# Four-layer graph network: another order ahead of the scatter, windows of 34, and an opening of the last layer without filler

## The chip, the cores and the metric

The kernel runs on one core of a Trainium2 chip. The metric is the device time of one execution in microseconds; the time before is the median of three runs. A core has five engines that work side by side and meet at semaphores: PE (matrix products into PSUM), DVE (vector), ACT (scalar, table functions), POOL (GpSimd) and SP, which here only issues transfers. PE's clock can be granted at 2.4 GHz (1.00 in the profile) or at half of it, 1.2 GHz (0.50).

## The reference

A graph of 625 nodes with 512 features and 20000 edges, sorted by destination, goes through four layers, each behind a layer norm and a ReLU, each added to its input:

```
h = relu(layernorm(x));  x = x + L0(h)   # GCN: D^-1/2 (A_w + I) D^-1/2 (h W_conv) + b_conv, then W_lin
h = relu(layernorm(x));  x = x + L1(h)   # SAGE: mean over in-edges @ W_l + b + h W_r, times its sigmoid
h = relu(layernorm(x));  x = x + L2(h)   # 4 transformer blocks: attention along edges + MLP,
                                         # norms conditioned on sin/cos of a noise level
h = relu(layernorm(x));  x = x + L3(h)   # GAT forward and backward, 4 heads each,
                                         # W_fuse, batch norm over nodes, relu
dst = min(int(625 * u**2), 9999), sorted # so low destinations have many edges
```

## The kernel before

All arrays stay in SBUF; nodes are padded to 640 and cut into five tiles of 128. Each engine has its own program, written out by hand in the order in which it shall run (`@block.vector`, `.scalar`, `.gpsimd`, `.tensor`, `.sync`); waits on semaphores are all that ties them. Nothing is scheduled by a planner. Products in fp32r are made of a high and a low half of each operand: ACT copies the high half (`high`), POOL subtracts it for the low half (`rest`, L1416), DVE does the same for activations.

**Preamble (0 to 33.7 us).** DVE turns the edge lists into columns, computes the norm of the five input tiles (`first_stats`, `first_norm`) and their low halves (`first_rest`), splits the edge weights into three bf16 parts (`w_part`, L2517 to L2520), and adds the bias row. ACT clears the accumulator, copies the turned tiles (`first_turned`, L1652), and computes the sine of the noise embedding. POOL computes the embedding's phase (in `mask`), the norms' inverse roots (`rstd_of`), the low halves of W_lin and W_conv, and adds the bias to x (L1464). PE turns the tiles and multiplies each by W_conv (`own_features`). SP loads the W_l and W_r tiles through a few staging slots.

**Scatter (33.7 to 118 us).** The dense weighted and unweighted adjacency is built as products of one-hot matrices. 40 groups of 512 edges: DVE makes three of the four source one-hots 128x628 (L2543), ACT the fourth (L1682, L1684), DVE the destination one-hot (L2545), `WIN` columns wide and relative to the group's lowest destination, POOL multiplies it by the three weight parts (L1483), PE makes 60 products per group (L2081 with 2 x WIN columns, twice L2084 with WIN), and DVE adds the 5 x 2 x WIN sums to the accumulator (L2554). The whole runs `passes + 1` times, passes = (widest group's span) / WIN.

**Behind it.** Degrees, their power -1/2 on POOL (L1498), scaled features, aggregation, W_lin, norm of layer 1, W_l and W_r, then the transformer blocks.

**Last layer (785.9 us on).** PE turns the mask, spreads rows of attention terms over partitions (L818), and makes the hidden features (`hidden`, 12 products each) of the forward direction. Then 8 x 5 items (n = 5 i + st): DVE the leaky-ReLU branches (L1040) and maxima (L1003) three heads ahead, POOL adds the mask (L632; for six items DVE), ACT exponentiates (L757), PE multiplies (L925) and frees the item's buffer; four buffers serve the first 15 items, six after. `idle_products` are products of a matrix of ones whose result nobody reads.

## Time and profile before

| | us |
|---|---|
| median of 3 runs | 902.62 |
| lowest, highest | 901.32, 902.70 |
| profiled execution, its own time | 900.32 |
| its span | 898.6 |
| PE busy in it | 837.1 (93%) |
| DVE busy | 644.9 (72%) |
| POOL busy | 516.5 (57%) |
| ACT busy | 459.7 (51%) |

The time of an execution and its span differ by 1.7 us, which lie outside the first and last instruction. Busy shares are averages over stages with different limits, so each edited stage has to be read by itself. The mean granted clock of PE is 0.988.

### The profile page before, as it was taken

How to read it: one execution, taken by the hardware profiler on the slowest of the kernel's cores; microseconds unless marked ns; L12 is line 12 of the kernel's file. 1: busy time of each engine (PE TensorE's matmuls, PEld its weight loads, DVE VectorE, ACT ScalarE, POOL GpSimd, SP SyncE). 2: the span in 40 equal slices, each digit the busy share in tenths (PEclk: the TensorE clock that was granted, in tenths of full speed). 3: DMA queues.
4: the chain of work that ended last, by engine and by line, in shares of the span. 5: the costliest groups of instructions: out<-in, count | busy, mean ns of one | idle time of the engine just before them, and what ended most of it. 6: DMA issues, size and time to landing. Idle time of an engine off the chain costs nothing.

```text
span 898.6 us, 18329 instructions
## 1 busy us (share of the span) xinstructions
PE 837.1 (93%) x6775; PEld 732.6 (82%) x6775; DVE 644.9 (72%) x1274; ACT 459.7 (51%) x771; POOL 516.5 (57%) x622
## 2 busy tenths in 40 slices
PE   3899999999999999999999999999999999998797
PEld 2798877779898878989887989888898988875466
DVE  8899988885575774476667366577546667689986
ACT  4787757244674233476134456424346634155664
POOL 7777744469532666743367853266684338447871
PEclk9999999999999999999999999999999999989989
DMA  5100011133200133300015310013230002100121
GB/s 135 37 0 0 0 48 26 60 102 110 59 2 5 31 109 91 109 13 2 12 44 159 89 54 12 1 36 98 81 113 20 1 1 83 36 1 31 45 60 58
DMA packets 49761, 44.34 MB, mean 49 GB/s; under 512 B 6013, under 2 KB 37439, under 8 KB 49698
## 3 DMA queue, kind: packets, MB, share of 16 engines
q1 hardware_dynamic: 47234, 39.72, 15.2%
q10 hardware_dynamic: 2464, 3.80, 1.5%
q8 instruction: 38, 0.62, 0.3%
q14 instruction: 25, 0.20, 0.1%
HBM read 42.04 MB, written 1.33 MB: 48 GB/s over the span
## 4 chain that ended last, share of the span: by engine, by line
PE 70%; DVE 16%; ACT 6%; issue 4%; DVEq 2%; POOL 1%; DMA 0%; SPq 0%; ACTq 0%
PE psum L1796 20%; PE psum L1790 18%; PE psum L1901 12%; PE psum L1871 6%; PE psum L1820 5%; PE psum L925 3%; DVE arena L2321 3%; ACT arena L1598 2%; PE psum L1844 2%; PE psum L866 1%; DVEq L2550 1%; DVE z L2543 1%; DVE arena L1003 1%; DVE stats L2444 1%; DVE hot_dst L2545 1%
## 5 line engine op out<-in xcount | busy, mean ns | idle before, releaser
L1345 POOL TENSOR_SCALAR acc<-acc,rden,flag 128x628 f32<-128x628 f32 x80 | 69.4, 868 | 119.4 <-DVE rden L2317 119.4
L1901 PE MATMUL psum<-ringw,arena 128*128 128x512 f32 (+1 forms) x480 | 119.3, 397 | 4.0 <-DVE arena L2329 2.5
L1796 PE MATMUL psum<-arena 128*128 128x384 f32 (+5 forms) x675 | 115.9, 325 | 1.1 <-DVE hot_dst L2694 1.1
L1790 PE MATMUL psum<-arena,ringw 128*128 128x314 f32 x768 | 114.2, 310 | 0.1
L1790 PEld LDWEIGHTS psum<-arena,ringw 128*128 128x128 f32 x768 | 112.9, 190 | 1.4 <-DVE arena L2294 1.1
L1796 PEld LDWEIGHTS psum<-arena 128*128 128x128 f32 (+1 forms) x675 | 104.9, 189 | 8.1 <-DVE hot_dst L2694 1.5
L1901 PEld LDWEIGHTS psum<-ringw,arena 128*128 128x128 f32 (+1 forms) x480 | 86.9, 186 | 25.6 <-DVE arena L2329 3.5
L1790 PE MATMUL psum<-arena 128*128 128x314 f32 (+1 forms) x480 | 87.8, 321 | 7.3 <-DVE arena L2321 6.7
L1790 PEld LDWEIGHTS psum<-arena 128*128 128x128 f32 (+1 forms) x480 | 70.4, 187 | 15.8 <-DVE arena L2321 14.1
L1416 POOL TENSOR_TENSOR ringw<-raw,ringw 128x512 fp32r<-128x512 f32 x56 | 71.7, 1291 | 19.3 <-ACT ringw L1639 15.4
L2294 DVE SCALAR_TENSOR_TENSOR arena<-psum,cols,arena 128x628 fp32r<-128x628 f32 x32 | 27.9, 871 | 70.6 <-ACT arena L1580 70.5
L1820 PE MATMUL psum<-ident,acc 128*128 128x128 f32 (+1 forms) x528 | 75.3, 274 | 0.2
L2321 DVE TENSOR_TENSOR arena<-psum,arena 128x640 fp32r<-128x640 f32 x80 | 65.0, 817 | 14.5 <-ACT arena L1598 14.5
L1416 POOL TENSOR_TENSOR ringw<-xn,ringw 128x512 fp32r<-128x512 f32 x49 | 64.9, 1329 | 16.2 <-ACT ringw L1639 16.1
L1483 POOL TENSOR_TENSOR hot_dst<-hot_dst,w_part 128x160 bf16<-128x160 bf16 x120 | 58.2, 512 | 26.2 <-DVE hot_dst L2545 26.2
L1593 ACT ACTIVATE acc<-acc,nsmax 128x628 f32<-128x628 f32 x80 | 65.2, 815 | 13.3 <-DVE nsmax L2312 12.9
L1820 PEld LDWEIGHTS psum<-ident,acc 128*128 128x128 f32 (+1 forms) x528 | 61.7, 140 | 8.0 <-DVE arena L2294 1.2
L1409 POOL TENSOR_SCALAR veps<-mv 128x1 f32<-128x1 f32 x60 | 13.6, 227 | 90.7 <-DVE mv L2448 89.0
L2312 DVE CUSTOM_DVE_ANT_0 acc<-psum,mask 128x628 f32<-128x628 f32 x80 | 63.7, 801 | 0.0
L1529 ACT ACTIVATE arena<-psum 128x512 fp32r<-128x512 f32 x40 | 23.8, 594 | 73.8 <-PE psum L1820 58.9
L1796 PE MATMUL psum<-arena,ringw 128*128 128x314 f32 x384 | 58.5, 310 | 2.3 <-DVE arena L2211 2.3
L1871 PE MATMUL psum<-ringw,arena 128*128 128x512 f32 x240 | 58.7, 395 | 0.9 <-DVE arena L2211 0.6
(310 smaller groups left out, 1907.0 us busy)
## 6 DMA issues: line engine op xcount, KB each, us to landing
raw<-in_L_gnn_m_w SPq DMA_DIRECT2D x16, 256.0 KB
xn<-in_L_gnn_m_w SPq DMA_DIRECT2D x16, 256.0 KB
raw<-in_L_gnn_wv SPq DMA_DIRECT2D x8, 256.0 KB
xn<-in_L_gnn_wv SPq DMA_DIRECT2D x8, 256.0 KB
raw<-in_L_gnn_wq SPq DMA_DIRECT2D x8, 256.0 KB
xn<-in_L_gnn_wq SPq DMA_DIRECT2D x8, 256.0 KB
raw<-in_L_gnn_wk SPq DMA_DIRECT2D x8, 256.0 KB
xn<-in_L_gnn_wk SPq DMA_DIRECT2D x8, 256.0 KB
```

Source lines behind the costliest of these rows:

```text
L1345: g.tensor_scalar(pbuf[:, k % 4, 0:NW], pbuf[:, k % 4, 0:NW], rden[:, k:k + 1], flag[:, 1, k % NT:k % NT + 1], ALU.mult, ALU.mult).then_in ...
L1416: g.tensor_tensor(to[1], staged[slot(n)], to[0].bitcast(F32), ALU.subtract).then_inc(split_done, 1)
L1483: ins = g.tensor_tensor(hot_dst[:, b, :, (i + 1) * WIN:(i + 2) * WIN], hot, w_part[:, i, :, bass.ds(gr, 1)].broadcast_to([P, CH, WIN]), AL ...
L1593: act.activation(pbuf[:, k % 4, 0:NW], pbuf[:, k % 4, 0:NW], ACT.Exp, bias=nsmax[:, k:k + 1], scale=-1.0, accum_out=den[:, k:k + 1]).then_ ...
L1790: ins = pe.matmul(big[buf(u)][0:l.shape[1], h, 0:HW], l, r[:, h * HW:(h + 1) * HW], start=(i == 0), stop=(i == len(terms) - 1))
L1796: ins = pe.matmul(to, l, r, start=(i == 0), stop=(i == len(terms) - 1))
L1820: ins = pe.transpose(bflat(u)[0:KEYS[k], k * P:(k + 1) * P], src[:, k * P:k * P + KEYS[k]], ident[:, :])
L1871: ins = pe.matmul(brow(u), l, r, start=(k == 0 and i == 0), stop=(k == KT - 1 and i == 2))
L1901: ins = pe.matmul(brow(ROWBLK[f"{name}{t}"])[0:KEYS[t], :], l, r, start=(pieces[0] + i == 0), stop=(pieces[-1] == KT - 1 and i == len(term ...
L2294: dve.scalar_tensor_tensor(wide(to[:, 1, h, :]), bwide(u), bqk[:, i, bass.ds(it * KT + h, 1)], wide(f32(to[:, 0, h, :])), ALU.add, ALU.sub ...
L2312: dve.tensor_tensor_reduce(wide(pbuf[:, k % 4, :]), bwide(u), wide(mask[:, t, :]), -DH ** -0.5, 3e38, ALU.add, ALU.min, nsmax[:, k:k + 1]) ...
L2321: dve.tensor_tensor(pT[:, 1, :, t * P:(t + 1) * P], bflat(u).rearrange("p (k n) -> p k n", k=NT), f32(pT[:, 0, :, t * P:(t + 1) * P]), ALU ...
```

## The change

- The window of a group is 34 destinations (`WIN`), the buffers keep room for 40 (`ROOM`).
- Preamble: POOL's sum of the phase waits for DVE's two small products; the low half of W_conv stands two steps earlier; the five bias additions leave for behind the scatter, two ahead of the degrees' power, three behind the last W_l halves. DVE splits the weights ahead of the bias row and the last two tiles, and no longer copies the diagonals (ACT does, with the ones and two W_l tiles, ahead of its third tile) nor waits for the own features before the loop. PE turns the fifth tile ahead of the embedding's product and the third own features. The W_r tiles load in another order, the first into z once the degrees are summed. Filler products: 4 becomes 2, 7 becomes 6, 1 becomes 3.
- Last layer: the fifth hidden tile stands in two halves of six products where seven products of ones stood; six of ones ahead of the loop become five; four stand at each of four places in the loop.

```diff
-WIN = 40
+WIN = 34
+ROOM = 40
...
-ACCW = NP + WIN
+ACCW = NP + ROOM
...                                            # last layer, PE
+                if p == NJ // 2 - 1:          # in target_rows(p), ahead of its wait on c_up
+                    idle_products(pe, 0, 4)
...
             hidden(3)
-
-            pe.wait_ge(h_read, 2 * NT - NROW)
-            spare = 2 * NBIG + ROW3[f"Hf{NT - 1}"] % NROW
-            idle_products(pe, spare, 1)
             target_rows(0)
-            idle_products(pe, spare, 3)
+            hidden(4, range(0, KT // 2))
             second_branch(0)
-            idle_products(pe, spare, 3)
+            hidden(4, range(KT // 2, KT))
             pe.wait_ge(am_read, 2)
             second_branch(1)
             first_branch(0)
             maxima(EARLY)
             first_branch(1)
-            hidden(4)
             pe.wait_ge(one_up, 2)
             pe.wait_ge(h_read, 2 * NT)
-            idle_products(pe, 2 * NBIG, 6)
+            idle_products(pe, 2 * NBIG, 5)
             for n in range(NJ * NT):
...
+                for p in range(1, NJ // 2):
+                    if n == 2 * NT * p - 5:
+                        pe.wait_ge(misc_read, MISC[f"vt{p}"] + 1)
+                        idle_products(pe, 0, 4)
                 pe.wait_ge(p_up, n + 1)
...                                            # SP, loads of W_r
-                elif n in Q_RIGHT[:2]:
-                    sp.wait_ge(xb_up, NT)
-                elif n >= OUTER:
+                elif n == Q_RIGHT[0]:
+                    sp.wait_ge(deg_full, 1)
+                elif n >= OUTER and n != Q_RIGHT[1]:
...                                            # POOL
             step(g.tensor_scalar(part, kf, -TURN_HI, 1.0, ALU.mult, ALU.mult))
+            g.wait_ge(dstep, 9)
             step(g.tensor_tensor(r, part, ph, ALU.add))
             rstd_of(0, 0)
             rstd_of(1, 1)
             rest(Q_LIN, ringpart(Q_LIN))
             step(g.tensor_scalar(part, kf, -float(2 * np.pi - TURN_HI), 1.0, ALU.mult, ALU.mult))
             rstd_of(2, 2)
+            rest(Q_CONV, ringpart(Q_CONV))
+            rstd_of(3, 3)
             step(g.tensor_tensor(r, r, part, ALU.add))
-            rstd_of(3, 3)
             g.tensor_scalar(r, r, 3.1415925, -3.1415925, ALU.min, ALU.max).then_inc(emb_up, 1)
             rstd_of(4, 4)
-            rest(Q_CONV, ringpart(Q_CONV))
...
             for k in range(2):
                 left_rest(k)
+            for t in range(2):
+                bias_added(t)
             g.wait_ge(w_up, 1)
...
             for k in range(2, KT):
                 left_rest(k)
+            for t in range(2, NT):
+                bias_added(t)
...                                            # ACT, behind first_turned(1)
+            act.wait_ge(scat_read, HOT)
+            act.wait_ge(scat_full, HOT)
...
+            act.activation(diag, ident[:, :].unsqueeze(1).broadcast_to([P, NT - 1, P]), ACT.Copy).then_inc(acc_up, 1)
+            act.activation(w_acc[:, NT - 1, (NT - 1) * P:NP], ident[:, :], ACT.Copy).then_inc(acc_up, 1)
+            act.activation(ones_r[:, :], ones[:, :], ACT.Copy).then_inc(ones_up, 1)
+            for m in range(2, 4):
+                high(m, ringpart(m)[0])
...                                            # DVE, ahead of the loop
-            dve.tensor_copy(diag, ident[:, :].unsqueeze(1).broadcast_to([P, NT - 1, P])).then_inc(acc_up, 1)
-            dve.tensor_copy(w_acc[:, NT - 1, (NT - 1) * P:NP], ident[:, :]).then_inc(acc_up, 1)
             dve.wait_ge(acc_up, 2)
             dve.wait_ge(w_ready, 2)
             dve.wait_ge(hot_init, 3)
-            dve.wait_ge(big_full, BIG0["hall"] + 1)
```

DVE ahead of the scatter loop, before (L2457 is a tile's norm, L2463 a turned tile's low half, L2514 the bias row, L2517 to L2520 the weight parts, L2531 and L2532 the diagonals):

```order
L2457 TENSOR_SCALAR xn<-x,mv,rstd 128x512
L2514 TENSOR_TENSOR bias<-psum,bias 128x512
L2463 SCALAR_TENSOR_TENSOR arena<-psum,arena 128x4x128
L2457 TENSOR_SCALAR xn<-x,mv,rstd 128x512
L2517 CAST w_part<-edge_col 128x160
L2519 TENSOR_TENSOR edge_col<-edge_col,w_part 128x160
L2520 CAST w_part<-edge_col 128x160
L2519 TENSOR_TENSOR edge_col<-edge_col,w_part 128x160
L2520 CAST w_part<-edge_col 128x160
L2463 SCALAR_TENSOR_TENSOR arena<-psum,arena 128x4x128 x2
L2531 COPY acc<-ident 128x4x128
L2532 COPY acc<-ident 128x128
```

The same place after (L2486 is the norm, L2492 the low half, L2550 the bias row, L2540 to L2543 the weight parts, L2555 a product for the condition):

```order
L2486 TENSOR_SCALAR xn<-x,mv,rstd 128x512
L2540 CAST w_part<-edge_col 128x160
L2542 TENSOR_TENSOR edge_col<-edge_col,w_part 128x160
L2543 CAST w_part<-edge_col 128x160
L2542 TENSOR_TENSOR edge_col<-edge_col,w_part 128x160
L2543 CAST w_part<-edge_col 128x160
L2550 TENSOR_TENSOR bias<-psum,bias 128x512
L2492 SCALAR_TENSOR_TENSOR arena<-psum,arena 128x4x128
L2486 TENSOR_SCALAR xn<-x,mv,rstd 128x512
L2492 SCALAR_TENSOR_TENSOR arena<-psum,arena 128x4x128
L2555 TENSOR_TENSOR pick<-fcol,pick 128x1
L2492 SCALAR_TENSOR_TENSOR arena<-psum,arena 128x4x128
```

The weight parts stand ahead of the bias row and the fifth norm, and the copies of the diagonal are gone.

PE at the opening of the last layer, before (L1796 hidden features, L1807 products of ones, L843 the turned target rows, L818 rows spread over partitions, L925 the weighted products of the loop):

```order
L1796 MATMUL psum<-ringw,arena 128x256 x12
L1807 MATMUL psum<-ones_r 128x512
L843 MATMUL psum<-ident,iota 36x128 x5
L1807 MATMUL psum<-ones_r 128x512 x3
L818 MATMUL psum<-arena 128x314 x2
L1807 MATMUL psum<-ones_r 128x512 x3
L818 MATMUL psum<-arena 128x314 x8
L1796 MATMUL psum<-ringw,arena 128x256 x12
L1807 MATMUL psum<-ones_r 128x512 x6
L925 MATMUL psum<-hot_dst,acc 128x314 x4
```

After (L821, L854, L827, L1834 and L935 in the same roles):

```order
L821 MATMUL psum<-ringw,arena 128x256 x12
L854 MATMUL psum<-ident,iota 36x128 x5
L821 MATMUL psum<-ringw,arena 128x256 x6
L827 MATMUL psum<-arena 128x314 x2
L821 MATMUL psum<-ringw,arena 128x256 x6
L827 MATMUL psum<-arena 128x314 x8
L1834 MATMUL psum<-ones_r 128x512 x5
L935 MATMUL psum<-hot_dst,acc 128x314 x4
```

The twelve products of the fifth tile stand around the second spread, and nothing but five products of ones is left between the last spread and the loop.

PE in the loop ahead of the last pair of heads, after:

```order
L935 MATMUL psum<-raw,acc 128x314 x2
L1834 MATMUL psum<-ones_r 128x512 x4
L854 MATMUL psum<-ident,iota 36x128 x5
L935 MATMUL psum<-hot_dst,acc 128x314 x2
L1834 MATMUL psum<-ones_r 128x512 x4
L935 MATMUL psum<-hot_dst,acc 128x314 x2
```

Both fours of L1834 are new there; the other rows keep their order.

## Rows read from the trace of the kernel before

**Rows 1.** The page's part 4, the chain by engine, share of the span.

```profile
PE 70%; DVE 16%; ACT 6%; issue 4%; DVEq 2%; POOL 1%; DMA 0%; SPq 0%; ACTq 0%
```

**Rows 2.** Busy time, ten scatter groups: PE, PEld, DVE, ACT, POOL, clock, DMA, GB/s.

```profile
61.08:81.40 20.32, 18.79 (x604) 18.01 (x601) 20.32 (x51) 15.37 (x21) 14.45 (x31) 1.00 0.00 0
```

**Rows 3.** Timeline, DVE ahead of the scatter: start, duration, engine, line, operation, [idle before].

```profile
8.97 1.57 DVE L2442 TENSOR_SCALAR xn<-ident,mnmx 40x40 f32<-40x40 f32 x1
...
23.89 1.21 DVE L2520 CAST w_part<-edge_col 128x160 bf16<-128x160 f32 x1
...
28.99 0.69 DVE L2463 SCALAR_TENSOR_TENSOR arena<-psum,arena 128x512 fp32r<-128x512 f32 x1 [0.73 <-ACT arena L1652]
...
33.72 0.97 DVE L2543 TENSOR_SCALAR mask<-iota,edge_col 128x628 bf16<-128x628 f16 x3 [2.92 <-issue]
```

**Rows 4.** Waits of DVE, 785 to 898 us: total, times, longest.

```profile
DVE hot_dst L1040 <- PE psum L925: 3.4, 3, 2.6
...
DVE raw L1040 <- PE psum L925: 0.6, 2, 0.4
```

**Rows 5.** Busy time of PE and granted clock, two stretches of the last layer.

```profile
802.90:809.70 6.80, 6.24 (x19) 0.51 0.00 1
854.00:860.60 6.60, 6.60 (x14) 0.50 0.42 128
```

**Rows 6.** Timeline, the other engines ahead of the scatter.

```profile
8.98 1.52 POOL L1441 TENSOR_TENSOR mask<-mask 64x640 f32<-64x640 f32 x1
...
21.54 1.28 POOL L1416 TENSOR_TENSOR ringw<-raw,ringw 128x512 fp32r<-128x512 f32 x1
...
23.62 6.41 POOL L1464 TENSOR_TENSOR x<-x,bias 128x512 f32<-128x512 f32 x5
...
22.97 2.05 PE L1796 MATMUL psum<-ringw,arena 128*128 128x256 f32 x8 [1.89 <-DVE arena L2463]
...
30.30 2.16 PE L1796 MATMUL psum<-ringw,arena 128*128 128x256 f32 x16
...
21.12 0.60 ACT L1652 ACTIVATE arena<-psum 128x512 fp32r<-128x512 f32 x1 [4.26 <-PE psum L1820]
...
28.29 0.60 ACT L1652 ACTIVATE arena<-psum 128x512 fp32r<-128x512 f32 x1 [1.78 <-PE psum L1820]
```

**Rows 7.** DMA issues to 130 us: count, KB each, median us to landing.

```profile
bias<-in_L_gnn_W_r SPq DMA_DIRECT2D x2, 256.0 KB, 2.8
```

**Rows 8.** Groups by line, DVE, 62 to 102 us: busy us, mean ns, idle before.

```profile
L2543 DVE TENSOR_SCALAR mask<-iota,edge_col 128x628 bf16<-128x628 f16 x30 | 14.0, 519 | 0.0
...
L2554 DVE TENSOR_TENSOR acc<-psum,acc 128x400 f32 x20 | 11.2, 560 | 0.0
L2545 DVE TENSOR_TENSOR hot_dst<-iota,edge_col 128x160 bf16<-128x160 f16 x20 | 6.2, 311 | 0.0
```

**Rows 9.** Timeline, POOL and DVE behind the scatter.

```profile
120.17 1.97 POOL L1498 TENSOR_TENSOR degs<-degs,half 128x2 f32<-128x2 f32 x2 [2.56 <-DVE degs L2609]
126.06 2.54 POOL L1416 TENSOR_TENSOR ringw<-raw,ringw 128x512 fp32r<-128x512 f32 x2 [3.92 <-DVE arena L2584]
...
132.69 0.51 DVE L2457 TENSOR_SCALAR xn<-x,mv,rstd 128x512 f32<-128x512 f32 x1
```

**Rows 10.** Timeline, opening of the last layer's loop: PE, ACT, POOL.

```profile
805.35 2.90 PE L1807 MATMUL psum<-ones_r 128*128 128x512 f32 x6 [0.56 <-ACT acc L659]
...
805.10 1.52 ACT L757 ACTIVATE hot_dst<-hot_dst,edge_col 128x628 f32<-128x628 f32 x2
...
802.38 3.02 POOL L632 TENSOR_TENSOR hot_dst<-hot_dst,acc 128x628 f32<-128x628 f32 x2 [1.50 <-issue]
```

**Rows 11.** Timeline, PE's gaps in the loop.

```profile
834.66 1.30 PE L925 MATMUL psum<-raw,acc 128*128 128x314 f32 x4 [2.04 <-ACT z L693]
...
849.32 0.71 PE L843 MATMUL psum<-ident,iota 128*36 128x128 f32 x5 [1.59 <-DVE iota L1025]
...
853.12 1.62 PE L925 MATMUL psum<-hot_dst,acc 128*128 128x314 f32 x4 [2.04 <-ACT z L693]
```

77 lines of the change are left out of this document (43 added, 34 removed).

## The prediction

> **What bounds the kernel now.** I read the page's chain of waits first, then busy time by stage, then the timeline of each engine around the edited places, and last who waited for whom and the granted clock. The chain is 70% PE, 16% DVE [rows 1]: over most of the run PE sets the pace, and the change does not touch that part. It touches three stages in which PE does not set the pace, and a short one behind the scatter.
>
> In the scatter (33.7 to 118 us) DVE has no idle time: in a stretch of ten groups it is busy 20.32 of 20.32 us, PE 18.79, ACT 15.37, POOL 14.45 [rows 2]. A group is 2.03 us of DVE. What starts DVE earlier, or makes a group of its work shorter, moves the end; PE has 0.15 us a group to spare.
>
> Ahead of the scatter DVE's last product of the preamble ends at 29.68 and its first scatter operation starts at 33.72 [rows 3]. In the last layer DVE stood still 2.6 us for a PE product at one place [rows 4], while PE ran at half clock [rows 5].
>
> **1. The start of the scatter.** Before, DVE goes: fifth tile's remainder at 28.99, diagonal copies until 30.80, then 2.92 us idle [rows 3]. That wait was for the own features, whose 16 products follow PE's own order; then the pass count is loaded. PE's last own-feature products start at 30.30 and take 2.16 [rows 6], to 32.46, so load and loop entry cost 33.72 - 32.46 = 1.26 us. After, the copies are ACT's, which has a 4.26 us gap where they go [rows 6], and the wait on the own features is gone. What is late next is the remainder of the fifth tile, which follows ACT's copy (28.29 + 0.60) [rows 6]. With nothing else moved the loop starts at 28.89 + 1.26 = 30.15, 3.6 us earlier.
>
> The fifth tile itself comes earlier. PE's first own-feature group stood 1.89 us before 22.97, because the conv weight's low half (POOL, 21.54 for 1.28) was late; from there to the fifth tile PE is never idle [rows 6]. POOL now does that half ahead of the wave's second sum, 1.28 us from about 16.5 on, so it is done by 17.8 and PE saves its 1.8 us. On DVE the fifth tile's norm is now behind the splitting of the weights, five operations on 128x160. Three of them took about 1.2 us each (the one at 23.89: 1.21) [rows 3], as long as one of POOL's bias additions, 6.41 for five [rows 6]. Those additions are moved behind the scatter. An operation of this size takes 0.31 in the loop [rows 8], so five cost about 1.5 us, and the norm is ready some 1.5 us later than before, near 24.6; ACT's copy, due at 28.29 - 1.8 = 26.5, needs it about 1 us ahead, for PE's four transposes. So both hold: 3.6 + 1.8 = 5.4; I take **-5.3**. Upper end of the gain: the new wait of POOL for DVE's two 40x40 products keeps its sum from lying on the second (8.97, 1.57 us, beside POOL's 8.98, 1.52) [rows 3, 6]; if the input had landed by then, DVE is up to 1.2 us earlier throughout: -6.5. Lower end: -3.0, if the fifth tile is not earlier and ACT, which now also copies two W_l tiles ahead of its third tile, is 0.6 late. The second W_l tile is requested once the conv half is done: 17.8 + 0.8 of issue + 2.8 to land [rows 7] = 21.4, against the third tile's 21.12 [rows 6]. One W_r load now goes into z and is requested only when the degrees are summed; ACT reads it behind four more copies and the features, so I cost it at nothing; if that cover is gone it is one landing, under 2.8 us.
>
> **2. Forty groups with 34 columns instead of 40.** Two DVE operations shrink: the addition from 128x400 to 128x340, the comparison from 128x160 to 128x136. The two rows give a slope: (560 - 311) / (400 - 160) = 1.04 ns an element [rows 8]. So 60 x 1.04 + 24 x 1.04 = 87 ns a group, 40 groups: -3.5 us. The three 128x628 operations keep their size, but not necessarily their time. Beside POOL's three multiplications they take 3 x 0.52 = 1.55 us [rows 8], at the start with POOL idle 0.97 [rows 3], so 0.58 a group is spent blocked. POOL's operations lose 15% of their elements; if all of the blocked time followed, that is 0.087 a group, -3.5 more. Most of a POOL operation of this size is probably fixed, so I take a quarter: **-4.4**, with ends -2.5 (POOL starts its first product sooner and gives some back) and -7.0. The other engines stay under DVE's 1.92: PE's 1.88 falls too, since its columns go from 160 to 136 a triple; ACT needs 1.54. The last groups drain about 0.3 us faster.
>
> The Trainium skill, "SBUF — State Buffer", "SBUF: two separate sides", says that DVE in a two-port mode and GpSimd exclude each other for the whole instruction. By that rule all of the blocked time would shrink with POOL's instruction, and the sum would be 886.6. The rows at 8.97 and 8.98 agree with it; the loop does not tell how much of a 0.48 us POOL operation is held.
>
> **3. Behind the scatter.** Five bias additions of 1.28 come back here. Two go into POOL's idle 2.56 us before the power of the degrees [rows 9]: 2 x 1.28 fills it exactly, and since the drain is 0.3 faster the power is late by about that, so this gain goes. Three follow the last W_l halves: 126.06 + 2.54 + 3.84 = 132.44, then the first variance's 0.8: 133.2 against DVE's norm at 132.69 [rows 9]. DVE is busy from there to 141, so +0.5 to the end; a small product taken out of DVE gives 0.2 back: **+0.3** (0 to +1.5).
>
> **4. Opening of the last layer.** Before: fifth tile's 12 products until 804.8, 0.56 us for ACT's copy, six products of ones 805.35 to 808.25 at half clock [rows 5, 10], and only then the first weighted product; DVE, out of buffers, waits 2.6 us for it [rows 4]. After, the twelve stand in two halves where seven products of ones stood, beside ACT's copies. Only five products of ones follow ACT's last copy, which is now due about 2.7 us before its 804.8, near 802.1; at half clock (2.90 / 6 each) they end by 804.5. POOL's first addition ends at 802.38 + 1.51, ACT's exponential takes 0.8 [rows 10], so the first weighted product can start at 804.8 against about 808.1: 3.3 earlier, more than DVE's 2.6. The whole stop goes: **-2.6**. Late next is POOL, 1.51 an item: its fourth ends at 808.4, and the fifth comes from the DVE operation that stood, so POOL follows it. Ends: -1.5 and -3.0.
>
> **5. Products of ones in the loop.** Before the last pair PE stands 1.59 and 2.04 us [rows 11], and from 854.0 it runs 6.6 us at 0.50, the 1.2 GHz level [rows 5]; DVE then waits for PE: 3.4 - 2.6 + 0.6 = 1.4 us in small stops [rows 4]. A single gap of 2.04 at 834.66 [rows 11] was followed by no fall. Four products of 0.2 now stand in each of the two gaps, which leaves 0.8 and 1.2. The later four wait for ACT's copy of the target rows, which in ACT's order stands ahead of the sums that release PE [rows 11], so they delay nothing. **-1.4** (0 to -2.4).
>
> Sum: -5.3 - 4.4 + 0.3 - 2.6 - 1.4 = -13.4. The profiled execution took 900.3 (span 898.6): 886.9. It lies 2.3 under the median shown, 902.6, to which the same sum gives **889.2**.
>
> **Rivals.**
> *The port lock in full*: term 2 is -7.0 instead of -4.4, 886.6; with term 1 at its end 885.4. For it: the three DVE products that took just one bias addition each [rows 3, 6].
> *The start is only half earlier*: ACT waits for the second W_l tile before its third tile and the sine behind it, or PE's own features are late. Term 1 is -3.0: 891.5. For it: the 21.4 against 21.12 above; against: the sine's table load has slack to the fourth tile.
> *The half clock stays*: PE's loop is thinner, the drain shorter; a stretch as at 854 stays or comes up elsewhere. Term 5 is 0 and one more stretch costs 1.4: 892.0.
> *Little is left*: the start at -3.0, the groups at -2.5, +1.5 behind them, -1.5 in the layer: 897.
> *A second pass (the slower side)*: the loop runs (widest group's span / WIN) + 1 times. Forty additions in the trace are one pass at 40. If a group of 512 edges reached from its lowest to its highest destination by 34 or more, all 40 groups run twice: 40 x 1.92 = 77 us, 966. The draw has density 16 edges a destination at the top, 512 / 16 = 32; computed from the reference's own draw the widest group spans 32. One or two destinations of margin decide, and they are there.
>
> **How the numbers follow.** Forecast with its own range 886.5 to 891: 0.52. Port lock 0.14, start half 0.13, half clock 0.12, little left 0.05, second pass or another slowing 0.04. Range 883.5 to 895.5: it holds all but the last two and some of the edges. A difference under 0.2% (1.8 us) could not be told from none. Faster 0.94: all cases but the last and a corner of "little". Same 0.02. Slower 0.04.
>
> **What would show it.** First DVE product of the loop near 28.4 (term 1); the weight splitting under 2 us in all. Period of a group 1.92, scatter's end near 108 (term 2). DVE's norm behind the scatter waiting under 1 us for POOL (term 3). No DVE stop over 0.5 us near the layer's opening, first weighted product 3 us after DVE's first branch (term 4). Clock 1.00 through the last ten items (term 5). Wrong would be: a loop start after 30, a period over 1.98, or 80 additions.

## The result, and the profile after

| | before | after |
|---|---|---|
| median of the runs shown with the result | 901.97 (4 runs) | 886.96 (4 runs) |
| profiled execution | 900.3 | 886.9 |
| its span | 898.6 | 885.2 |
| mean granted clock of TensorE in it | 0.988 | 0.995 |

All times are in us. The ratio is 0.9848, 95% interval 0.9813 to 0.9882: the changed kernel is 15 us faster. Beside experiments 5, 6 and 7 below it ran again: 886.18, six runs from 885.90 to 888.44, ratio 0.9840 (0.9813 to 0.9866). The ten runs together have a median of 886.6, and that is what "the changed kernel" means below. Forecast was 889.2, with a range of 883.5 to 895.5. The forecast's sum of -13.4, put on the profiled execution, gave 886.9, and that is what the profiled execution took; the median moved by 15.0, not by 13.4. The agreement to the tenth is in part luck, as the terms at the end show.

The chain of waits of the changed kernel, by engine. PE has lost five points of it [rows 1]:

```profile
PE 65%; DVE 18%; ACT 5%; issue 4%; DVEq 3%; DMA 2%; POOL 1%; SPq 0%; POOLq 0%; ACTq 0%
```

Ten groups of the scatter after the change, columns as in [rows 2]. They take 19.00 us where they took 20.32. DVE is still busy all the time, PE 18.37 of 19.00, so DVE sets the pace as before:

```profile
61.03:80.03 19.00, 18.37 (x616) 17.62 (x613) 19.00 (x52) 15.48 (x21) 13.37 (x31) 1.00 0.00 0
```

The timeline of DVE ahead of the scatter, after. These rows answer to [rows 3]:

```profile
9.18 0.23 DVE L2471 TENSOR_SCALAR xn<-ident,mnmx 40x40 f32<-40x40 f32 x1
10.43 0.69 DVE L2473 BATCH_NORM_STATS2 stats<-x 128x6 f32<-128x512 f32 x1 [1.02 <-DMA x<-in_x]
...
18.55 1.71 DVE L2486 TENSOR_SCALAR xn<-x,mv,rstd 128x512 f32<-128x512 f32 x1
...
22.03 0.24 DVE L2540 CAST w_part<-edge_col 128x160 bf16<-128x160 f32 x1
...
26.70 0.69 DVE L2492 SCALAR_TENSOR_TENSOR arena<-psum,arena 128x512 fp32r<-128x512 f32 x1 [0.30 <-ACT arena L1673]
27.95 0.97 DVE L2566 TENSOR_SCALAR mask<-iota,edge_col 128x628 bf16<-128x628 f16 x3 [0.55 <-issue]
```

The loop starts at 27.95 instead of 33.72. The cast at 22.03 takes 0.24 where one at 23.89 took 1.21 with POOL's bias additions beside it. The 40x40 product is down from 1.57 to 0.23, but DVE then waits 1.02 for its input: the first statistics start at 10.43 where they started at 10.57, so 0.14 of it arrives further on. A collision has grown: the norm at 18.55 takes 1.71. The same norm took 0.90 before (at 18.96, beside a POOL operation of 0.71 that started at 18.86), and the norms with nothing beside them take 0.54. The timeline of POOL shows the longer operation that it now meets; the norm ends 0.29 after it. Further on PE waits 0.63 for DVE's fifth norm (24.65) before it turns the fifth tile:

```profile
18.44 1.53 POOL L1465 TENSOR_TENSOR mask<-mask 64x640 f32<-64x640 f32 x1
...
25.34 0.63 PE L1847 MATMUL psum<-ident,xn 128*128 128x128 f32 x4 [0.63 <-DVE xn L2486]
```

DVE behind the scatter waits for POOL's root, which now stands behind three bias additions (timeline of POOL and DVE; the row at 132.69 of [rows 9] had no wait):

```profile
117.58 3.80 POOL L1481 TENSOR_TENSOR x<-x,bias 128x512 f32<-128x512 f32 x3
...
121.74 0.56 POOL L1426 TENSOR_TENSOR rstd<-veps,half 128x1 f32<-128x1 f32 x1
...
122.33 0.55 DVE L2486 TENSOR_SCALAR xn<-x,mv,rstd 128x512 f32<-128x512 f32 x1 [0.54 <-POOL rstd L1426]
```

The opening of the last layer: DVE's fifth item starts at 797.42, right behind what comes before it, where in the kernel before it stood 2.6 us [rows 4]:

```profile
797.42 0.87 DVE L1050 SCALAR_TENSOR_TENSOR hot_dst<-psum,edge_col,bias 128x628 f32<-128x628 f32 x1
```

The timeline of PE there: five products of ones, a wait of 1.21 for ACT, and the first weighted product at 794.88, 3.5 us after DVE's first branch (791.38):

```profile
792.25 1.43 PE L1834 MATMUL psum<-ones_r 128*128 128x512 f32 x5
794.88 3.97 PE L935 MATMUL psum<-hot_dst,acc 128*128 128x314 f32 x8 [1.21 <-ACT hot_dst L761]
```

The busy time of the last layer by stage shows the granted clock. Between 790 and 870 it falls once, in the opening, and no longer behind 810 [rows 5 had 0.50 from 854.00 to 860.60]. It falls again from 880 on, when the engines have next to nothing left and only the output is stored; the trace of the kernel before has the same from 895 on, and it costs nothing. The last row is from a view of PE alone (its columns: length, PE, clock, DMA, GB/s):

```profile
790.00:800.00 10.00, 8.72 (x31) 5.61 (x30) 9.66 (x21) 4.93 (x9) 8.38 (x6) 0.83 0.00 1
800.00:810.00 10.00, 9.28 (x36) 5.67 (x37) 9.38 (x22) 6.90 (x10) 8.17 (x6) 1.00 0.21 61
810.00:830.00 20.00, 18.61 (x68) 10.76 (x67) 19.70 (x43) 13.58 (x21) 17.33 (x12) 1.00 0.18 52
830.00:850.00 20.00, 17.51 (x64) 10.61 (x65) 19.83 (x31) 13.94 (x22) 16.43 (x11) 1.00 0.20 53
850.00:870.00 20.00, 18.17 (x94) 14.63 (x93) 18.39 (x18) 11.69 (x18) 9.50 (x6) 1.00 0.08 18
...
880.00:882.00 2.00, 0.33 (x3) 0.51 0.98 314
```

### The profile page after: what moved, and what is told of

The parts are those of the page before. It is cut to its first block, busy times and chain, and to the rows that moved or that the text cites. A ratio compares the mean times of both kernels' runs of the same rounds, so it can differ in the third digit from the quotient of the medians.

```text
span 885.2 us, 18341 instructions
## 1 busy us (share of the span) xinstructions
PE 831.0 (94%) x6782; PEld 726.4 (82%) x6782; DVE 636.3 (72%) x1272; ACT 460.2 (52%) x773; POOL 510.8 (58%) x622
## 3 DMA queue, kind: packets, MB, share of 16 engines
HBM read 42.04 MB, written 1.33 MB: 49 GB/s over the span
## 4 chain that ended last, share of the span: by engine, by line
PE 65%; DVE 18%; ACT 5%; issue 4%; DVEq 3%; DMA 2%; POOL 1%; SPq 0%; POOLq 0%; ACTq 0%
PE psum L1823 19%; PE psum L1817 18%; PE psum L1928 13%; PE psum L1898 6%; PE psum L1847 5%; DVE arena L2350 3%; ACT arena L1619 2%; DVEq L2573 2%; DVE arena L1013 2%; PE psum L1871 2%; PE psum L935 2%; DVE z L2566 1%; PE psum L877 1%; DVE mask L2566 1%; DVE stats L2473 1%
## 5 line engine op out<-in xcount | busy, mean ns | idle before, releaser
L1817 PE MATMUL psum<-arena 128*128 128x314 f32 (+1 forms) x480 | 87.8, 321 | 7.3 <-DVE arena L2350 6.8
L1817 PEld LDWEIGHTS psum<-arena 128*128 128x128 f32 (+1 forms) x480 | 70.5, 187 | 15.9 <-DVE arena L2350 14.1
L1500 POOL TENSOR_TENSOR hot_dst<-hot_dst,w_part 128x136 bf16<-128x136 bf16 x120 | 53.1, 469 | 24.7 <-DVE hot_dst L2568 24.7
```

The lines of the kernel that those rows point to most:

```text
L1500: ins = g.tensor_tensor(hot_dst[:, b, :, (i + 1) * WIN:(i + 2) * WIN], hot, w_part[:, i, :, bass.ds(gr, 1)].broadcast_to([P, CH, WIN]), AL ...
L1817: ins = pe.matmul(big[buf(u)][0:l.shape[1], h, 0:HW], l, r[:, h * HW:(h + 1) * HW], start=(i == 0), stop=(i == len(terms) - 1))
```

## How the runs are compared

The median of six runs moves by a microsecond or two, and the granted clock differs between runs of one kernel. The experiments were timed in three groups on three chips (1 to 4; 5, 6, 7 and the changed kernel; 8 to 11), in which the kernel before had medians of 901.43, 900.92 and 902.12, so times of different groups compare to about a microsecond. The traces are finer, if read at fixed places of DVE. Each kernel's profiled execution gives six: start of the scatter loop; start of the last addition of a window; first norm behind the scatter; first branch of the last layer; its fifth item; the span.

| kernel | loop | last addition | norm | first branch | fifth item | span |
|---|---|---|---|---|---|---|
| before | 33.72 | 117.69 | 132.69 | 801.38 | 810.07 | 898.6 |
| changed | 27.95 | 106.42 | 122.33 | 791.38 | 797.42 | 885.2 |
| changed, again | 27.76 | 106.21 | 122.13 | 791.03 | 797.08 | 884.4 |
| 1. windows of 40 | 27.76 | 111.86 | 127.91 | 796.83 | 802.88 | 891.3 |
| 2. only the windows | 34.31 | 112.76 | 127.69 | 796.50 | 803.73 | 891.1 |
| 3. last layer undone | 27.71 | 106.11 | 122.03 | 790.95 | 800.65 | 888.5 |
| 4. no ones in the loop | 28.31 | 106.78 | 122.69 | 791.56 | 797.61 | 893.6 |
| 5. opening undone | 27.55 | 106.01 | 121.92 | 790.89 | 796.94 | 884.1 |
| 6. weights later | 27.50 | 105.94 | 121.86 | 790.82 | 796.86 | 885.4 |
| 7. bias ahead | 28.29 | 108.86 | 123.64 | 792.54 | 798.59 | 885.9 |
| 8. wait at the entry | 31.13 | 109.83 | 125.75 | 794.63 | 800.67 | 888.4 |
| 9. only the loop's ones | 33.57 | 117.66 | 132.65 | 801.48 | 808.54 | 895.8 |
| 10. three more edits | 27.96 | 105.27 | 120.52 | 789.82 | 795.87 | 883.7 |

From the norm to the first branch, where the change moves only some loads of W_r and two filler products, every kernel takes 668.7 to 669.3. So a difference at the norm is still there at the last layer.

## The experiments

### 1 and 2. The windows, put back and alone

```diff
# 1: changed kernel
-WIN = 34
+WIN = 40
# 2: kernel before
-WIN = 40
+WIN = 34
+ROOM = 40     # the buffers keep their size
```

Expected of the first: 

> The changed kernel with one number put back: windows of 40 destinations in place of 34, everything else as changed. Theory A (fewer elements and less of VectorE's time held up beside GpSimd's larger products): a group takes 2.03 to 2.04 us again in place of 1.90, the scatter grows by the 5.6 us that the two traces differ by over its 40 groups, 887.0 becomes 892.6, and nothing behind the scatter moves. Rival B (elements alone, 84 fewer at 1.04 ns each, 3.5 us over 40 groups, and the other 2 us come from the new order ahead of the loop, for example no half clock of TensorE at its start): the group shrinks by 0.087 us only and the time is 890.5. Rival C (the wait behind the scatter for the bias additions eats part of what the windows gave, since a later end hides it): about 892.0, and the norm's wait for GpSimd of 0.54 us stays at 0.5 in A and goes in C.

Measured: 892.87, six runs from 891.66 to 893.55, which is 6.3 above the changed kernel. The loop starts where it did (27.76) and the last addition is at 111.86 instead of 106.21: 5.65 us. Behind it, last addition to norm is 16.05, as in the changed kernel (15.92). Theory A holds in its place and in its amount, and B's 3.5 is too little. C is out too: the norm behind the scatter still waits 0.56 for POOL.

Expected of the second: 

> The kernel before with windows of 34 destinations and nothing else of the change. Theory A (the windows' gain stands by itself): 902.0 - 5.6 = 896.4, the group at 1.90 us from the second one on. Rival B (part of the gain belongs to the new order): 902.0 - 3.5 = 898.5. In A the norm behind the scatter waits no longer for GpSimd than before (its bias additions are still ahead of the scatter), so the end keeps the whole gain.

Measured: 895.59, twelve runs from 890.36 to 898.03, against 901.43 in the same comparison; ratio 0.9932 (0.9909 to 0.9954). From loop start to last addition it takes 78.45, as the changed kernel does, where the kernel before takes 83.97: 5.5 us. The gain stands by itself and does not need the new order.

The place where the time comes from is one group of DVE. First the kernel with windows of 40, then the changed one (timeline: start, duration, engine, line, operation):

```profile
61.34 1.40 DVE L2566 TENSOR_SCALAR mask<-iota,edge_col 128x628 bf16<-128x628 f16 x3
62.66 0.32 DVE L2568 TENSOR_TENSOR hot_dst<-iota,edge_col 128x160 bf16<-128x160 f16 x1
62.90 0.56 DVE L2577 TENSOR_TENSOR acc<-psum,acc 128x400 f32 x1
63.38 1.40 DVE L2566 TENSOR_SCALAR z<-iota,edge_col 128x628 bf16<-128x628 f16 x3
```

```profile
61.03 1.34 DVE L2566 TENSOR_SCALAR z<-iota,edge_col 128x628 bf16<-128x628 f16 x3
62.29 0.29 DVE L2568 TENSOR_TENSOR hot_dst<-iota,edge_col 128x136 bf16<-128x136 f16 x1
62.50 0.50 DVE L2577 TENSOR_TENSOR acc<-psum,acc 128x340 f32 x1
62.92 1.34 DVE L2566 TENSOR_SCALAR z<-iota,edge_col 128x628 bf16<-128x628 f16 x3
```

Read from start to start: the three masks take 1.26 instead of 1.32, the comparison 0.21 instead of 0.24, the addition 0.42 instead of 0.48. Comparison and addition give the 0.087 us of the slope [rows 8]; the masks, whose size is unchanged, give 0.055 more on average over the 26 and 28 groups between 46 and 100 us. POOL's three multiplications beside them went from 1.45 to 1.33 us, so the masks got back about half of what POOL's operations lost. Measured against what the masks are held up, it is more: three masks take 0.97 with POOL idle [rows 3], 1.40 beside POOL with 40 columns and 1.34 with 34, so the part held up went from 0.43 to 0.37, by about 13%, where POOL's operations have 15% fewer elements.

### 3, 4 and 5. The last layer: all of it undone, only the loop's ones, only the opening

```diff
# 4 (changed kernel): no products of ones in the loop
-                if p == NJ // 2 - 1:
-                    idle_products(pe, 0, 4)
...
-                for p in range(1, NJ // 2):
-                    if n == 2 * NT * p - 5:
-                        pe.wait_ge(misc_read, MISC[f"vt{p}"] + 1)
-                        idle_products(pe, 0, 4)
# 5 (changed kernel): the opening as before
...
+            idle_products(pe, spare, 1)
             target_rows(0)
-            hidden(4, range(0, KT // 2))
+            idle_products(pe, spare, 3)
             second_branch(0)
-            hidden(4, range(KT // 2, KT))
+            idle_products(pe, spare, 3)
...
             first_branch(1)
+            hidden(4)
...
-            idle_products(pe, 2 * NBIG, 5)
+            idle_products(pe, 2 * NBIG, 6)
...                                            # 5, ScalarE
             second_branch(0)
-            hidden("f", 3)
             second_branch(1)
-            hidden("f", 4)
+            for t in range(3, NT):
+                hidden("f", t)
# 3: both
```

The piece of ScalarE belongs to the change as well, though its list above leaves it out: the fourth hidden tile is copied between the two second branches.

Expected of 3: 

> The changed kernel with the last layer as it was: its fifth tile whole behind the first branches, the products of ones ahead of it, none in the loop. Theory A (the two traces: 2.65 us at the opening, where VectorE stood 2.6 us at its fourth branch, and 0.75 us in the loop and behind): 887.0 + 3.4 = 890.4, with the stop of 2.6 us and the second stretch at half the clock back near 844 us. Rival B (the forecast's own terms, 2.6 and 1.4): 891.0. Rival C (the loop is set by VectorE from both sides and takes up most of the stop): under 889.0, the stop is back and the span grows by less than 2 us.

Expected of 4: 

> The changed kernel without the three sets of four products of ones in the last layer's loop, and nothing else. Theory A (they keep the clock up where the pair of heads is turned; without them a stretch of some 6 us at half the clock stands near 840 to 850 us as before, and costs 1.4 us by the gaps of TensorE before): 888.4. Theory A', as the two traces sum up: 0.75 us, 887.7. Rival B (the clock stays up without them, since the opening is denser now and the loop starts elsewhere): 887.0, granted clock 1.00 from 800 to 870 us. Rival C (they cost TensorE more than they give): 886.5, with the clock low and still no later end, because VectorE and ScalarE set the loop's pace.

Expected of 5: 

> The changed kernel with the opening of the last layer alone as before (products of ones ahead of the second branches, the fifth tile whole behind the first ones), the products of ones in the loop kept. Theory A (the stop of VectorE at its fifth item is worth what it was in the two traces): 887.0 + 2.65 = 889.6; with the stop of 3.57 us that stands in the trace with the whole layer undone, 890.6. No half clock past 810 us. Rival B (the opening's stop is taken up in the loop, where VectorE waits for TensorE anyway): under 888.3, the stop is there and the loop is shorter by as much. Rival C (the old opening also makes the clock fall more often later): runs spread over 5 us or more with mean clocks down to 0.985.

| | median | runs | mean clock of the runs |
|---|---|---|---|
| 3. both undone | 889.26 | 887.3, 887.5, 888.3, 890.3, 890.7, 893.4 | 0.988 to 0.994 |
| 4. no ones in the loop | 890.86 | 886.7, 887.7, 888.3, 893.4, 895.3, 895.9 | 0.993 to 0.996, then 0.984 to 0.986 |
| 5. opening undone | 886.74 | 885.9, 886.4, 886.5, 887.0, 887.6, 890.3 | 0.995 to 0.999, the last 0.989 |
| changed, 10 runs | 886.6 | 885.9 to 887.0, two at 888.4 and 889.0 | 0.993 to 0.999 |

None of the theories had the form of this right: a kernel does not have one time here but two or three. The profiled execution of kernel 3 came out as theory A said (890.26 against 890.4), with both of A's marks in its trace, a stop (3.6 us) and a second fall near 846; its median, 889.26, lies between A and the bound of C. Kernel 5 missed A by 3 us, since its trace has no stop at all; its median is in the range of rival B, but B's mechanism, a stop that the loop takes up, is not what the trace shows. Kernel 4 has three runs about as fast as the changed kernel (rival B) and three that are 7 to 9 us longer, which no theory gave. Its profiled execution is one of the long ones. That both pieces undone give a shorter median than one of them (889.26 against 890.86) says how coarse medians of six such runs are: the two intervals overlap. Busy time by stretch with the granted clock, and PE's timeline ahead of both falls:

```profile
806.00:820.00 14.00, 13.42 (x31) 8.01 (x32) 9.19 (x18) 6.76 (x11) 8.83 (x7) 0.63 0.15 48
828.00:836.00 8.00, 8.00 (x18) 4.42 (x18) 4.43 (x11) 3.47 (x6) 5.45 (x4) 0.57 0.45 124
```

```profile
806.58 1.42 PE L929 MATMUL psum<-hot_dst,acc 128*128 128x314 f32 x4 [1.91 <-ACT z L697]
...
810.99 2.30 PE L929 MATMUL psum<-raw,acc 128*128 128x314 f32 x4
...
827.78 2.12 PE L929 MATMUL psum<-raw,acc 128*128 128x314 f32 x4 [1.91 <-ACT z L697]
```

Each time PE stands 1.91 us and soon after runs at half clock: four products take 2.30 where four others in this trace take 1.22. DVE, busy 19.70 of 20.00 us in the changed kernel's 810 to 830, is down to 9.19 of 14.00 and 4.43 of 8.00. From the fifth item to the end this execution takes 96.0 us, the changed kernel's 87.8 and 87.3. Such a gap is not enough for a fall: in kernel 3 PE stands 1.91 us ahead of 808.55 and 2.03 ahead of 825.78 and the clock stays, as it did behind the 2.04 of [rows 11] at 834.66. And not every fall costs as much: kernels 2 and 3, with a fall of some 3.4 us near 848 and near 846, take 87.4 and 87.9 over the same distance. Kernels 3 and 5 have the same code for the opening, word for word, and show what the clock does there. First 3, then 5, timeline of PE:

```profile
792.12 2.93 PE L821 MATMUL psum<-ringw,arena 128*128 128x256 f32 x12
795.61 2.90 PE L1833 MATMUL psum<-ones_r 128*128 128x512 f32 x6 [0.56 <-ACT acc L663]
798.31 3.92 PE L934 MATMUL psum<-hot_dst,acc 128*128 128x314 f32 x8
```

```profile
791.75 1.70 PE L821 MATMUL psum<-ringw,arena 128*128 128x256 f32 x12
794.01 1.63 PE L1839 MATMUL psum<-ones_r 128*128 128x512 f32 x6 [0.56 <-ACT acc L663]
795.48 2.28 PE L940 MATMUL psum<-hot_dst,acc 128*128 128x314 f32 x8
```

and the stretch 790 to 800 of each, with the clock:

```profile
790.00:800.00 10.00, 9.36 (x31) 7.25 (x31) 6.78 (x14) 4.29 (x7) 6.44 (x5) 0.57 0.00 1
```

```profile
790.00:800.00 10.00, 9.37 (x43) 6.83 (x44) 9.57 (x22) 5.08 (x8) 7.88 (x6) 1.00 0.00 1
```

In 3 the clock fell and DVE stopped 3.6 us at the fifth item; in 5 it did not fall and there is no stop. So the old order does not by itself stop DVE: it takes the fall too. With the old opening in five traces the time at half clock between 790 and 810 was 10.2, 6.8, 3.4, 3.4 and 0 us, and the stop 3.57, 2.57, 1.10, 0.92 and 0 (kernels 3, before, 2, 9 and 5). With the new opening it was 3.4 or 6.8 us in all eight traces (the changed kernel twice, 1, 4, 6, 7, 8 and 10; kernel 4 has its next fall on top), and DVE never stopped at the fifth item. The stop of kernel 3:

```profile
800.65 0.87 DVE L1049 SCALAR_TENSOR_TENSOR hot_dst<-psum,edge_col,bias 128x628 f32<-128x628 f32 x1 [3.57 <-PE psum L934]
```

What follows: the new opening removes the stop that a fall causes, 0 to 3.6 us by run, and not the fall. A small price is left: from the fifth item to the end the two traces with ones in the loop and a fall of 6.8 us (kernels 1 and 6) take 88.4 and 88.5, the others 87.2 to 87.8. The ones in the loop remove the falls behind 806, which cost 8 us in the one execution of kernel 4 that was profiled. No trace with the ones has a fall between 806 and 870, and each of the four without them has one or two. The runs without a trace agree by their mean clock: it is under 0.989 in 32 of the 69 runs of kernels without the ones (before, 2, 3, 4) and in none of the 60 with them.

### The changed kernel again, and 9. The loop's ones alone on the kernel before

```diff
# 9: kernel before, with the two pieces that experiment 4 takes out
```

Expected of the changed kernel: 

> The changed kernel as it is, timed on the same chip as the three beside it. Theory A (the products of ones in the last layer's loop keep TensorE from falling to half its clock there in every run): all six runs within 2.5 us of each other around 887, each with a mean granted clock of 0.993 or more. Rival B (the clock falls by chance in some runs of this kernel too, as in three of six without those products): some runs at 893 to 896 with a mean clock near 0.985.

Expected of 9: 

> The kernel before with the products of ones in the last layer's loop and nothing else of the change. Theory A (they keep TensorE's clock up from 820 to 880 us, and the falls there are what spreads the runs of the kernel before from 897.5 to 904): median 898.0 to 899.0, mean clocks of 0.992 or more in most runs, no half clock between 830 and 885 us. Rival B (the forecast's 1.4 us alone): 900. Rival C (the falls belong to the opening of the last layer, which is as before): 901.0 and the same spread.

The changed kernel: 885.90 to 888.44, 2.54 us from end to end, clock 0.994 to 0.999, as theory A had it but for 0.04 us. Kernel 9: 899.28, twelve runs from 896.01 to 900.59, clock 0.991 to 0.996, against 902.12 of the kernel before in 17 runs from 897.64 to 904.41; ratio 0.9974 (0.9954 to 0.9995). That is 2.8 us, twice the forecast's term and just short of A's 3.1 to 4.1. The interval runs from 0.5 to 4.1 us, so the time alone does not exclude B's 1.4; the mean clocks are what A said, and the spread of 4.6 us against 6.8 speaks against C. Busy time by stage in its trace, where the kernel before shows 0.83 for 850 to 870:

```profile
830.00:850.00 20.00, 17.66 (x65) 10.18 (x63) 19.70 (x40) 13.33 (x19) 18.04 (x12) 1.00 0.18 51
850.00:870.00 20.00, 18.11 (x71) 12.05 (x72) 20.00 (x24) 16.11 (x25) 16.75 (x10) 1.00 0.26 67
```

The 45 runs of the kernel before that stood beside the experiments fall in groups by their mean clock: nine at 0.992 and 0.993 average 897.7, twelve at 0.990 average 900.9, fifteen at 0.988 average 902.3, six at 0.986 average 904.2. None of the twelve runs of kernel 9 and of the changed kernel's ten is under 0.991; of the kernel before, 24 of 45 are under 0.990. That the long runs have their falls where the trace of kernel 4 has them is inferred, since only one execution of each kernel was traced. A mean clock also counts falls that cost nothing: the kernel before and kernels 2, 7, 8 and 9 run some microseconds at half clock in the first groups of the scatter, and from loop start to last addition kernel 2 takes 78.45 with it, the changed kernel 78.45 without.

### 6, 7 and 8. What moved the start of the scatter

```diff
# 6 (changed kernel): the weights' splitting behind the fifth tile's norm
-            ...five instructions on w_part, ahead of the bias row
             first_rest(2)
             first_norm(4)
+            ...the same five
             first_rest(3)
# 7 (changed kernel): GpSimd's bias additions ahead of the scatter again
+            for t in range(NT):
+                bias_added(t)
             g.wait_ge(sin_done, 2)
...
-            for t in range(2):
-                bias_added(t)
...
-            for t in range(2, NT):
-                bias_added(t)
# 8 (changed kernel): VectorE's wait back
             dve.wait_ge(hot_init, 3)
+            dve.wait_ge(big_full, BIG0["hall"] + 1)
             passes = dve.value_load(...)
```

Expected of 6: 

> The changed kernel with the five instructions that split the edges' weights put back behind the fifth tile's norm, the bias additions of GpSimd kept behind the scatter. Theory A (the 4.4 us that they took before were GpSimd's bias additions beside them, so their place is worth nothing by itself): they take 1.4 to 1.6 us there too, the fifth tile's norm stands 1.4 us earlier, TensorE's wait of 0.63 us for it goes, and the loop starts 0.3 to 0.6 us earlier or as now: 886.4 to 887.0. Rival B (their place was the gain): they take over 3 us and the loop starts 1.5 to 3 us later: 888.5 to 890. Rival C (VectorE now has these five behind ScalarE's copies, where it used to wait 0.45 and 0.30 us, so it only changes which it waits for): loop start within 0.2 us of 27.95, 887.0.

Measured: 887.06 (885.70 to 888.69), as the changed kernel within what six runs can tell. The five instructions take 1.5 us there too (23.48 to 25.00), the norm stands at 23.03 instead of 24.46 in the changed kernel of the same comparison, PE's wait is gone, and the loop starts 0.26 earlier. Theory A holds: their place was worth nothing, the 4.4 us that they took before are gone with POOL's bias additions beside them.

Expected of 7: 

> The changed kernel with GpSimd's five bias additions put back ahead of the scatter, the weights' splitting kept early. Theory A (they hold VectorE up where both run, and GpSimd's first products stand behind them): they end near 31 us, GpSimd's first products begin some 2 us later than 29.3, the first groups of the scatter wait for them, and of this 1 to 3 us stay at the scatter's end; behind it the norm's wait of 0.54 us for GpSimd goes: 887.5 to 889.5. Rival B (the scatter has four buffers and takes the late products up; nothing is left but the gain behind it): the scatter's last addition at 106.4 as now, 886.4. Rival C (the whole 3 us by which the weights' splitting was longer come back on other instructions of VectorE): loop start at 30 to 31 us, 889.5 to 890.

Measured: 888.22 (887.68 to 889.12), 1.6 above the changed kernel and 2.0 above its six runs of the same comparison. Timelines of DVE at the loop's start and of POOL:

```profile
28.29 2.94 DVE L2565 TENSOR_SCALAR mask<-iota,edge_col 128x628 bf16<-128x628 f16 x3 [0.56 <-issue]
```

```profile
23.96 6.51 POOL L1481 TENSOR_TENSOR x<-x,bias 128x512 f32<-128x512 f32 x5 [1.84 <-DVE bias L2549]
...
32.13 2.04 POOL L1503 TENSOR_TENSOR hot_dst<-hot_dst,w_part 128x136 bf16<-128x136 bf16 x4 [1.08 <-DVE hot_dst L2567]
```

The first three masks take 2.94 instead of 0.97. The last addition is 2.65 later than in the changed kernel. Behind the scatter the norm no longer waits, and addition to norm is 14.78 instead of 15.92: 1.1 comes back. At the first branch 1.5 is left. Theory A, in place and amount; the four buffers do not take it up (B), and the collision did move to other instructions (C), for the most part to the masks; ahead of them the fifth norm takes 1.22 instead of 0.54, and the loop starts 0.5 later, not 3.

Expected of 8: 

> The changed kernel with one wait put back ahead of VectorE's read of the number of passes: it waits for TensorE's last own features, as before the change; nothing else. Theory A (the loop start moved because this wait went, the rest ahead of it only let VectorE be there in time): TensorE's last own features end near 30.2 us, the loop starts 1.3 us behind at 31.5 in place of 27.8, and the scatter's end moves by the same 3.5 to 3.7 us: 889.7 to 890.2. Rival B (the first four groups run ahead of TensorE anyway, and TensorE is held by its own features till then, so a later VectorE is partly hidden): the last addition moves by under 2 us, 888.2 or less. Rival C (the trace's later order hides a wait of another kind, and the loop start stays within 0.5 us): 886.5.

Measured: 890.36 (889.83 to 892.06), 3.8 above. The loop starts 3.4 later, the last addition 3.6 later:

```profile
31.13 0.97 DVE L2567 TENSOR_SCALAR mask<-iota,edge_col 128x628 bf16<-128x628 f16 x3 [4.06 <-issue]
```

Theory A: the wait for TensorE's own features was the larger part of the later start, and VectorE's head start over TensorE hides none of it. Of the 5.8 us at the loop's start the wait holds 3.4; with it in place the loop starts 2.6 earlier than before (33.72 - 31.13), because PE ends its own features at 29.88 instead of 32.46. The distance to the loop is 1.25 here, 1.26 before.

### 10. Three more edits

```diff
-WIN = 34
+WIN = 33
# experiment 6, and on GpSimd:
-            for t in range(2, NT):
+            for t in range(2, 4):
                 bias_added(t)
-            for t in range(NT):
+            rstd_of(LN_L1, NT)
+            bias_added(4)
+            for t in range(1, NT):
                 rstd_of(LN_L1 + t, NT + t)
```

Expected: 

> The changed kernel with three further edits: the weights' splitting behind the fifth tile's norm (0.26 us earlier at the loop by the trace of it alone), GpSimd's bias additions of tiles 3 and 4 ahead of the first root behind the scatter and that of tile 5 behind it (the norm's wait of 0.54 us for the root goes, 0.5 us), and windows of 33 (14 elements less at 1.04 ns and half of what GpSimd's products lose, 0.9 us over 40 groups). Theory A: the sum, 1.7 us below the changed kernel's 886.2, 884.5; a group takes 1.875 us. Rival B (an odd width costs VectorE or GpSimd a slower form): the group at 1.92 us or more, 886.5 or more. Rival C (the root comes earlier but VectorE then waits for tile 5's addition, and TensorE is not later or earlier behind the scatter): 885.0.

Measured: 885.58, six runs from 884.93 to 886.19; the ratio to before is 0.9827 (0.9799 to 0.9856), that of the changed kernel 0.9840 (0.9813 to 0.9866), so the times alone do not tell the two apart. The timeline of DVE does:

```profile
60.48 1.33 DVE L2568 TENSOR_SCALAR z<-iota,edge_col 128x628 bf16<-128x628 f16 x3
61.73 0.29 DVE L2570 TENSOR_TENSOR hot_dst<-iota,edge_col 128x132 bf16<-128x132 f16 x1
61.93 0.49 DVE L2579 TENSOR_TENSOR acc<-psum,acc 128x330 f32 x1
62.34 1.33 DVE L2568 TENSOR_SCALAR z<-iota,edge_col 128x628 bf16<-128x628 f16 x3
...
120.52 0.86 DVE L2488 TENSOR_SCALAR xn<-x,mv,rstd 128x512 f32<-128x512 f32 x1
```

A group takes 1.86, so an odd width costs nothing here (against B). The median is 1.1 above theory A's 884.5. The norm waits no longer, though it takes 0.86 instead of 0.55 beside POOL's last bias addition. From loop start to first branch it is 761.86 against 763.27 of the changed kernel: 1.4 us, the sum of 0.5 and 0.9 that was expected, but not by these parts: 1.1 in the scatter, 0.7 behind it, and 0.4 lost between the norm and the first branch. The third part (0.26 at the loop's start) did not show, the loop started at 27.96. By the spans (883.7 against 885.2 and 884.4) this kernel is about a microsecond below the changed one.

### 11. Windows of 32

```diff
-WIN = 34
+WIN = 32
```

Expected: 

> The changed kernel with windows of 32 destinations, one number. The widest group of this input covers 32 and the program takes one pass for every full 32, so it now runs the scatter twice. Theory A (rival of the forecast, a second pass over all 40 groups): 40 times 1.86 = 74 us and some 3 us of entry more: 961 to 966. Rival B (a pass over groups that have nothing left is as dear but hides the loads behind it): 955 to 960. Rival C (one pass is enough): 885.

Measured: 961.97, two runs of 961.53 and 962.41. The timeline of DVE shows the first pass end and the second begin:

```profile
104.34 0.49 DVE L2577 TENSOR_TENSOR acc<-psum,acc 128x320 f32 x1 [0.77 <-PE psum L2113]
...
105.52 0.97 DVE L2566 TENSOR_SCALAR mask<-iota,edge_col 128x628 bf16<-128x628 f16 x3 [0.61 <-DVE base_i L2593]
```

Theory A: 75.4 us more than the changed kernel. The rival of the forecast was real, and begins one column below the narrowest width that was run in one pass.

## Why the prediction was right, term by term

**Start of the scatter, -5.3 forecast.** At the loop's start it was -5.8. The way there was right in its main part: the wait for the own features held it (experiment 8, 3.4 us), PE's earlier end gave the rest, and from the start of DVE's last product to the loop it took 27.95 - 26.70 = 1.25. The forecast read its 1.26 from the end of PE's own features, which experiment 8 repeats (1.25), and applied it to the end of ACT's copy, from where it is 27.95 - 26.60 = 1.35. Two details were off. The 40x40 product did lose its 1.2 us, which the upper end counted as a possible gain, and the input's arrival took back all but 0.14. And moving the bias additions was worth more than free weights: in experiment 7 it shows as 2.65 us at the scatter's end, though the splitting itself stayed short.

**Windows, -4.4 forecast.** It was -5.5 to -5.65 (experiments 1 and 2). The elements were right to the hundredth, 0.087 us a group. The mis-sized part is the time that the masks spend held up by POOL. The forecast put it at 0.58 us a group, but 1.55 is the sum of three overlapping records and 0.97 the time of three together; like against like it is 1.40 - 0.97 = 0.43. All of it shrinking by POOL's 15% of the elements would give 0.065 a group, so the rival in full should have been -6.1 and not -7.0. A quarter of 0.087 was assumed, 0.02 a group; 0.055 came. The wait is nearer to the rival's mechanism than to the forecast's quarter. The Trainium skill, "SBUF — State Buffer", "SBUF: two separate sides", has the loser of the shared ports wait for the whole instruction of the other. The norm at 18.55 agrees (1.71 us beside POOL's 1.53, 0.54 alone, its end 0.29 behind POOL's). In the loop the masks are held 0.43 beside 1.45 us of POOL; how the three instructions of each engine take turns there no run shows.

**Behind the scatter, +0.3 forecast.** From last addition to norm it was +0.9 (15.0 before, 15.9 after), and experiment 7, with the additions ahead of the scatter again, is 1.1 shorter there. Right in the place (the norm waits 0.54 for POOL) and short in the amount. The traces give two parts: the conversion behind the last addition takes 0.67 instead of 0.16 under a bias addition, which makes what follows 0.3 late, and the norm stands 0.6 later behind the work ahead of it.

**Opening of the last layer, -2.6 forecast.** In the two traces the fifth item came 2.65 earlier relative to the first branch (8.69 before, 6.04 after). The cause named in the forecast was incomplete: it took the twelve products and the ones in DVE's way as what is late, and the half clock as given in every run. Experiments 3 and 5 show that the same old order stops DVE 3.6 us in one run and not at all in another. So the term is 0 to -3.6 by run, and with the ones in the loop the median of the old opening is only 0.1 us above the changed kernel's (886.74 against 886.6). That the term matches the traces is luck of the execution that was profiled before.

**Products of ones in the loop, -1.4 forecast.** Between the fifth item and the end the two traces differ by 0.75. Over many runs the ones are worth 2.8 us on the kernel before (0.5 to 4.1), and 4.3 in the median on the changed one (890.86 against 886.6, six runs in two groups), in the form of long runs that no longer occur. The forecast had the mechanism and priced it by one profiled execution. For the two pieces of the last layer together, forecast at -4.0, the medians give -2.7 (889.26 against 886.6) and the two traces -3.4.

**The sum.** In the two traces the terms are -5.8, -5.5, +0.9, -2.65 and -0.75, and +0.4 between the norm and the first branch, for which the forecast had no term: -13.4. The start and the windows gave 1.6 more than forecast, the rest 1.6 less. That the sum came out to the tenth is luck.

**The step that failed** is the one behind the sum: "It lies 2.3 under the median shown, 902.6, to which the same sum gives 889.2". The distance of a median from one profiled execution is not a constant that a change leaves alone. About half of the 2.3 was the draw of three runs: over 45 runs the kernel before has a median of 901.4, 1.1 above its profiled execution. The rest goes, as far as the mean clocks show it, with the falls of the clock in some runs, which the change makes rarer: the changed kernel's profiled execution stands 0.3 above its median of 886.6. From median to median the change is worth 14.8 us by these runs, 1.4 more than by the traces.

## What to carry to other kernels

A wait at a loop's entry on the engine that sets the pace cost its full length here (3.4 us at the entry, 3.6 at the loop's end), so ask what the first iterations truly need. When one order gives runs in groups, compare the granted clock of each run before pricing a stop: here a stop of 2.6 us in one trace was 0.1 in the median, and products of ones priced at 0.75 by the traces were worth 2.8. And where one engine holds another up, making the one's work smaller gave the other back part of the time; measure it with the one number changed and everything else kept, and compare durations that are counted the same way.

## What the runs showed of the hardware

- TensorE's clock fell in one execution and not in another at the same place of the same code: 0.57 and 1.00 mean from 790 to 800 in kernels 3 and 5, which are alike up to there. Two levels were seen, 1.2 and 2.4 GHz. Ahead of the falls of kernel 4 the engine had stood 1.91 us; in kernel 5, with four products of ones (1.20 us together) in that gap, 0.43 and 0.41 us of it were left and the clock did not fall. Gaps of 1.91 and 2.03 us in kernel 3 were followed by no fall, and the fall at its opening had no such gap ahead of it, so a gap alone does not decide.
- GpSimd's operations hold VectorE's up only in part in the scatter loop: three masks take 0.97 us beside an idle GpSimd and 1.40 beside 1.45 us of it, and 0.12 us off GpSimd's three operations gave them 0.055. An instruction of 1.53 us on GpSimd made one of 0.54 on VectorE take 1.71.
- Widths of 40, 34 and 33 columns gave groups of 2.04, 1.90 and 1.86 to 1.87 us; the odd one is no slower.
